# Sorting all five edge groups of layer 1 in a two-layer graph kernel, with dense work on x beside the first sort

## The reference, cut to what matters

```python
edge_index = jnp.stack([src, dst]); batch0 = jnp.zeros((6250,), jnp.int32)
h = relu(layernorm(x))
# first layer (layer 1 below)
agg = zeros_like(h).at[src].add(edge_attr)                  # 100000 rows of 256
q = (h @ Wq.T + bq).reshape(n, H, DH); k, v = u[batch] @ Wk.T + bk, u[batch] @ Wv.T + bv
w = softmax(sum(q * k, -1, keepdims=True) / sqrt(DH), axis=-1)
cond = (w * v).reshape(n, D) @ Wo.T + bo
x = x + relu(concat([h, agg, cond], 1) @ W1.T + b1) @ W2.T + b2
# second layer
h = relu(layernorm(x))
ht = relu(h @ W1 + b1); w = exp(w_param)
fsum = segment_sum(sigmoid(w * ht[src] + b_param), dst, 6250)   # rows gathered by src, summed by dst
s = clip(fsum, 1e-6, 0.9999999); c = (log(s / (1 - s)) - b_param) / w
bundle = concat([ht, c], 1) @ Wn + bn
out = x + relu(bundle / max(norm(bundle), 1e-12))
```

## Time and profile before

| | us |
|---|---|
| median of three timed runs | 2949.75 (2943.0 to 2951.38) |
| the profiled execution | 2918.7 |
| its span | 2917.0 |
| TensorE busy (share of the span) | 2107.8 (72%) |
| VectorE busy | 1824.2 (63%) |
| GpSimd busy | 1787.9 (61%) |
| ScalarE busy | 1288.0 (44%) |
| mean granted clock of TensorE | 0.836 |

### The profile page before, as it was taken

The page is one execution under the profiler, slowest core; times in us unless marked ns, Lnnn a source line. Parts: engine busy times, 40 slices in busy tenths (PEclk is TensorE's granted clock), DMA queues, the critical chain, the costliest instruction groups (busy, mean ns, idle before and its releaser), DMA issues.

```text
span 2917.0 us, 36909 instructions
## 1 busy us (share of the span) xinstructions
PE 2107.8 (72%) x9923; PEld 1483.2 (51%) x9923; DVE 1824.2 (63%) x4995; ACT 1288.0 (44%) x4284; POOL 1787.9 (61%) x1714
## 2 busy tenths in 40 slices
PE   1569976677776877867997576777776777676785
PEld 0457754454554554545776354445455455443474
DVE  1574434665775775767775476677577677552586
ACT  0124443335444634635346343643553553463554
POOL 1577777767666666664025666666667667666337
PEclk9778886779887988988998687997888888885798
DMA  9888878435433333332546333333333333333143
GB/s 383 236 174 179 174 120 243 112 91 145 120 89 89 92 89 88 92 90 63 177 157 231 91 87 89 90 92 90 90 90 91 90 90 91 91 92 92 47 156 113
DMA packets 175359, 357.77 MB, mean 123 GB/s; under 512 B 32444, under 2 KB 100822, under 8 KB 172581
## 3 DMA queue, kind: packets, MB, share of 16 engines
q0 software_dynamic: 93168, 219.39, 30.0%
q1 hardware_dynamic: 70791, 101.03, 10.7%
q10 hardware_dynamic: 11200, 35.00, 3.2%
HBM read 275.21 MB, written 93.19 MB: 126 GB/s over the span
## 4 chain that ended last, share of the span: by engine, by line
PE 46%; DVE 23%; issue 12%; another core or an unknown queue 9%; SPq 3%; ACT 2%; DVEq 1%; POOL 1%; DMA 1%; POOLq 0%; ACTq 0%
PE bank L1405 44%; DVE agg L1171 11%; DVE oh L1103 3%; DVE hits L1099 3%; DVE store L1095 2%; SPq L452 1%; DVEq L1163 1%; ACT oh L791 1%; DVE cum L1056 1%; PE bank L1568 1%; SPq L480 1%; DVE store L904 1%; DVE cum L1063 1%; ACT store L719 0%
## 5 line engine op out<-in xcount | busy, mean ns | idle before, releaser
L1405 PE MATMUL bank<-store,oh 125*128 125x157 f16 (+2 forms) x6770 | 1530.0, 376 | 550.4 <-issue 213.4
L1405 PEld LDWEIGHTS bank<-store,oh 125*128 125x128 f16 (+1 forms) x6770 | 1012.9, 174 | 1003.4 <-issue 522.8
L1171 DVE TENSOR_TENSOR agg<-bank,agg 128x256 f32 x1845 | 777.4, 421 | 500.3 <-PE bank L1405 221.0
L646 POOL DMA_INDIRECT store<-g_table,idx_all x785 | 771.1, 982 | 386.1 <-issue 189.2
L791 ACT ACTIVATE oh<-dist 128x128 f32<-128x128 f32 x1845 | 499.1, 301 | 1079.4 <-PE bank L1405 610.9
L646 POOL DMA_INDIRECT store<-in_edge_attr,idx_all x628 | 626.1, 997 | 288.7 <-issue 144.8
L783 ACT ACTIVATE dist<-iota,nloc_all 128x128 f32<-128x128 f32 x1845 | 582.6, 386 | 74.0 <-DVE nloc_all L1143 38.2
L1095 DVE TENSOR_TENSOR store<-iota,ttab 125x628 f16<-125x628 f16 x360 | 173.4, 482 | 302.5 <-remote 210.6
L620 POOL DMA_INDIRECT agg_copy<-agg x160 | 251.8, 1574 | 173.5 <-ACT agg L746 79.4
L1103 DVE TENSOR_TENSOR oh<-hits,v 125x512 f16<-125x512 f16 x720 | 289.7, 422 | 6.4
L1405 PE MATMUL bank<-agg 128*128 128x256 f32 (+2 forms) x480 | 128.2, 419 | 55.3 <-DVE agg L1192 43.9
(11 more groups left out here) (207 smaller groups left out, 1512.1 us busy)
## 6 DMA issues: line engine op xcount, KB each, us to landing
agg_copy<-store ACTq DMA_DIRECT2D x4, 6400.0 KB
agg<-in_edge_attr SPq DMA_DIRECT2D x39, 512.0 KB, 4.3
store<-in_x SPq DMA_DIRECT2D x72, 256.0 KB
agg_copy<-agg_copy POOLq DMA_DIRECT2D x16, 800.0 KB
store<-g_table,idx_all POOLq DMA_INDIRECT x785
store<-in_edge_attr,idx_all POOLq DMA_INDIRECT x628
pre_scratch<-store SPq DMA_DIRECT2D x25, 256.0 KB
agg<-agg_copy SPq DMA_DIRECT2D x25, 256.0 KB
```

What stands on the lines that cost most here:

```text
L646: gp.indirect_dma_start(out=store[:, at % RING * D:(at % RING + 1) * D], out_offset=None, in_=table_dram, in_offset=bass.IndirectOffsetOnA ...
L1171: dve.tensor_tensor(to, pt[n % TB][:, 0:D], to, ALU.add).wait_op(s_mm, n + 1, "sem-ge").then_inc(s_acc, 1)
L1405: return pe.matmul(o, l, r, start=start, stop=stop, skip_group_check=skip)
```

## The change

It does five things.

1. Layer 1 has five sorted groups and no scattered one (SPREAD goes, G1 = 5, SORTS = 10). All the buffers, transfers and instructions of the scatter and of the folds go.
2. Stage A has 27 blocks (START = NW + 2). The weights are prepared ahead of the first, so ahead of the sort too. Block b has the dense work of chunk b (b < 25) and an even share of the first sort's atoms.
3. x is loaded once for stage A, straight to `agg`, which holds it until GpSimd clears each chunk after its transpose. The normalisation coefficients are made by batches of five chunks (`ln_coefs`, `norms_ready`).
4. The product of ht with the upper half of Wn, with bn added by a product of ones, is made in 50 halves between the jobs of stage D (`upper_product`, at the steps of HT_STEPS: six in each of the first four groups, 26 in the last), copied out by ScalarE and stored as `q_dram`.
5. In stage E the lower half of Wn is scaled once by 1/w, `bundle_product` has two products a row block, VectorE adds the stored half and clamps, ScalarE takes squares with a fixed scale, the per-row maximum goes, and VectorE does the scaled relu nine chunks later (`positive`) in GpSimd's place.

The core of the diff:

```diff
-SPREAD = 1
-G1 = GROUPS - SPREAD
+G1 = GROUPS
...
-        BLOCKS = spread_over([1.0] * (WBLOCK + 1) + [2.0] * (FIRST - WBLOCK - 1) + [0.76] * (EBLKS - 2 - FIRST)) + [range(0)] * 2
+        BLOCKS = spread_over([1.0] * START)
+        HT_STEPS = [(g, t) for g in STAGES[1][:-1] for t in (50, 54, 58, 147, 151, 155)]
+        HT_STEPS += [(STAGES[1][-1], 4 + 6 * i) for i in range(2 * NW - len(HT_STEPS))]
+        HT_HALF = {at: divmod(i, 2) for i, at in enumerate(HT_STEPS)}
...   # SP, stage D
+            upper_load(0)
+            for g in STAGES[1]:
+                for t in range(TILES):
+                    if (g, t) in UPPER_STORES:
+                        upper_store(UPPER_STORES[g, t])
+                    if (g, t) in HT_HALF and HT_HALF[g, t][1] and HT_HALF[g, t][0] + 1 < NW:
+                        upper_load(HT_HALF[g, t][0] + 1)
+                    if PLACE_ATOM + 3 in atoms_at(1, g, t):
+                        column_starts(g + 1)
...   # GpSimd, stage A
+            for n in range(NW):
+                gp.wait_ge(s_tp, n + 1)
+                gp.memset(slot2k(agg, n), 0.0).then_inc(s_z, 1)
...   # ScalarE, stage A
+            weights_ready()
+            norms_ready(0)
+            norm_relu(0)
+            for b in range(START):
+                if 1 <= b <= NW:
+                    act.wait_ge(s_d, b)
+                    act.activation(soft[:, 1, (b - 1) % 2, :], soft[:, 0, (b - 1) % 2, :], ACT.Exp).then_inc(s_e, 1)
+                if b < NW:
+                    h_out(b)
+                if 1 <= b <= NW:
+                    weights_out(b - 1)
+                    pre_out(b - 1)
+                if b + 1 < NW:
+                    if (b + 1) % CHB == 0:
+                        norms_ready((b + 1) // CHB)
+                    norm_relu(b + 1)
...   # VectorE, stage A
+            weights_ready()
+            ln_coefs(0, 2 * CHB, 1)
+            for b in range(START):
                 atoms = BLOCKS[b]
                 half = len(atoms) // 2
+                if 1 <= b <= NW:
+                    weights(b - 1)
                 for k in atoms[:half]:
                     sort_atom(0, k)
+                if b < NW:
+                    scores(b)
                 for k in atoms[half:]:
                     sort_atom(0, k)
+                if b + CHB < NW:
+                    stats(b + CHB)
+                    if b % CHB == CHB - 1:
+                        dve.wait_ge(s_bn0, b + CHB + 1)
+                        ln_coefs(2 * (b + 1), 2 * (b + 1 + CHB), b // CHB + 2)
...   # TensorE, stage A
+            for b in range(START):
                 atoms = BLOCKS[b]
                 half = len(atoms) // 2
+                if b < NW:
+                    h_transpose(b)
+                if 1 <= b <= NW:
+                    weight_transpose(b - 1)
                 for k in atoms[:half]:
                     sort_atom(0, k)
+                if b < NW:
+                    h_product(b)
+                if 1 <= b <= NW:
+                    weighted(b - 1)
+                if b < NW:
+                    score_product(b)
                 for k in atoms[half:]:
                     sort_atom(0, k)
+
+            def upper_product(n, j):
+                pe.wait_ge(s_hl, 16 * (n + 1))
+                if n >= 2:
+                    pe.wait_ge(s_qo, n - 1)
+                to = (pA, pB)[n % 2][:, j * D:(j + 1) * D]
+                for k in range(KD):
+                    mm(to, w1bT[:, k * WIN + j * P:k * WIN + (j + 1) * P], wn[:, k, :], k == 0, False)
+                r = mm(to, ones[0:1, :], bnbc[0:1, :], False, True)
+                if j:
+                    r.then_inc(s_qp, 1)
...   # VectorE, stage E
             def bundle(n):
                 dve.wait_ge(s_bm, n + CHB + 1)
+                dve.wait_ge(s_xl[n % CHB], XLOADS + 16 * (n // CHB) + 16)
+                dve.tensor_tensor(agg[:, n * CH:(n + 1) * CH], pt[n % CHB % 2][:, :], slot2k(ring, CHB + n % CHB),
+                                  ALU.add).then_inc(s_bs, 1)
+                dve.wait_ge(s_bs, n + 1)
+                ts(agg[:, n * CH:(n + 1) * CH], agg[:, n * CH:(n + 1) * CH], BMAX, -BMAX, ALU.min, ALU.max).then_inc(s_bd, 1)
```

More of the change, by code:

```diff
@@ L1385, in _ @@
                     norm_out(n // CHB - 1)
+                if n >= OUT_LAG:
+                    positive(n - OUT_LAG)
             bundle(NW - 1)
-            scale(NW - 1)
+            for n in range(NW - OUT_LAG, LASTS):
+                positive(n)
             norm_in(CBODIES - 1)
```

574 lines of the change are left out of this document (158 added, 416 removed).

## The result

The changed kernel takes **3026.51 us** (median of four runs, 3021.69 to 3028.99) against 2946.38 (2942.52 to 2951.38) for the kernel before: a ratio of 1.0274, with a 95% interval of 1.0256 to 1.0291. The forecast was 3017 us, the range 2975 to 3065. The profiled execution took 3021.69 us, its span is 3019.6.

What follows compares the result with a forecast made beforehand. No one engine bounds the whole: TensorE paces the dense work, the ring of gathers the sorted groups. Terms -130 + 226 - 1.5 + 3 - 30 = +67.5 us gave 3017 us, range 2975 to 3065.

Steps and rivals of the forecast that it cites:

- Stage A: Start, first sort and dense work on x: without the scatter, gathers start near 304 us instead of 434.4, -130 us.
- The turn of 9.7 us: Dense loop of stage A: VectorE's 3.7 us and TensorE's 6.0 us per chunk run in series.
- Rival 1: Stage A's turn is TensorE's work alone, 7.0 us; gathers start at 222, total 2935 us; chance 0.07.
- rival 4: TensorE's clock falls in stage A; at 0.73 the turn is 10.9 us, total 3046 us; chance 0.14.
- The four coefficient places: Stage A, after chunks 4, 9, 14, 19: coefficients and a table load delay VectorE 5 us each, 20 us.
- Stage B: Layer 1's sorted groups: a fifth costs 231.5 us less about 5 for dropped fold transfers, +226 us.
- Stage C: Dense work between the layers: fold sums and loads go, only the head is gained, -1.5 us (0 to -5).
- Stage D: Layer 2's five sorted groups: the upper product added in their loops costs +3 us (-3 to +25).
- The ring of gathers hides it: Stage D: gathers pace each group, so the upper product's 75 us on TensorE are covered.
- Rival 2: Upper product's halves run in series in stage D: +75 to +87 us, 3089 us or more; chance 0.07.
- Stage E: The end: less VectorE work per chunk and a shorter tail, -30 us (-18 to -38).
- Rival 3: The end doesn't give its 30 us, as chunks wait for ScalarE's logarithms and table loads: 3047 us; chance 0.1.

Runs made afterwards that it cites:

- The filler: The changed kernel with five extra constant transposes on TensorE per chunk in stage A: 2678.2 us against 2695.59 on the same chip.
- the two other orders: Two kernels, each the changed kernel with one edit: weights' transpose moved behind the chunk product, 2682.71 us; all statistics and coefficients ahead of the loop, 2673.22 us.
- the orders together: The changed kernel with both the later weights' transpose and the statistics and coefficients ahead of the loop: 2997.69 us against 3027.08.

## Why the prediction was right, point by point

**Stage A (-130, came -124.3).** The weight preparation was put at 20 to 36 us and ran from 23.3 to 38.4. The first weights' reciprocal came at 50.3, the last at 301.7. The first scores came at 48.7 (forecast 44) and the last at 299.1 (294), so the loop took its 250 us, and 5 of the 6 us that the gathers came late are in the start. The turn of 9.7 us was right in its mechanism, VectorE and TensorE in series, and nearly in its sum: 9.76 to 9.79 in the even turns, 10.05 on average in the middle of the stage. The runs bear the mechanism out: taking the transpose out of the series gave turns down to 7.0, the rival's value for TensorE alone, and the gathers came 20 us earlier. Rival 1 with its 222 us was never near, since TensorE has other work between, and even with both costs gone it needs 8.0 a turn.

The clock was the weak step, and here luck helped. I took 0.88 from a stretch in which TensorE was full and applied it to one in which I had found it busy 6.9 of 9.7 us. It was 0.71 to 0.74: rival 4's condition came true. Its gathers at 333 did not, because its turn of 10.9 us was worked out with 5.3 us for TensorE at full clock and 3.7 for VectorE. TensorE's part is 4.8 at full clock and became 6.4 to 6.5 at the clock it was granted, VectorE's is 3.3 to 3.7. Work put too high and a clock put too high cancelled: with the right clock and the work as I had it the forecast would have been rival 4's. The filler shows a reserve of 21 us in stage A; each of the two other orders gives about as much, 20 and 25 us, and the orders together only 27.

The four coefficient places were put at 5 us each. VectorE's part of those turns is 7.9 to 8.5 us instead of 3.3, 4.5 to 5.2 more each. As whole turns they stand 6.4, 6.1, 4.3 and 4.3 us above the average of 10.05, 21 us for 20; the first two have a slower part of TensorE besides.

**Stage B (+226, in this pair +245.4).** The term was a group at 231.5 less 5 for the folds, which have no row behind them. The price by timed runs is 237.8, so the term was mis-sized by 6. Half of it I put down to the source: its length came from a profiled execution that was 28 us quicker than the median. Over nine groups that is 3 us a group, which I should have added, having noted the difference and put all differences on the median unscaled. That it lies in the groups is worked out, not shown: the middle groups of the changed kernel and of its variants on 2946 chips last 234 to 238 us, those of the kernel before, as profiled, 230.5 to 235.5. A second trace of the kernel before on a 2946 chip would tell, and the one that was meant to came from a 2670 chip. So the rival, that the changed kernel's groups are longer by their own doing, isn't excluded. The sign that I had given, groups of 230 to 233 us in B, did not come: the five are 232 to 236.

**Stage C (-1.5, came -4.8).** At the better end of its bounds.

**Stage D (+3, in this pair +21.2).** 9.6 us of it are the upper product's, within the bounds of -3 to +25 but not the +3 taken. The rest, 12 us, I put down to the quick profile of the kernel before as in B, five groups at 2 to 3 us, which is not shown either. In this pair a middle group of D grew by 3 to 6 us, on average 4.5: more than the 3 that I had called right, and once more than the 5 that I had called wrong; 1 to 2 us of that are the product's, by the run without it. "The ring of gathers hides it" is right on the 2670 chips (0.1 us between traces of one chip, 1.8 between those of the changed kernel and the kernel before on two) and only nearly right on the 2946 chips. Rival 2 (75 to 87 us in series) falls.

**Stage E (-30, came -34.9).** A chunk went from 4.8 to 3.96 us (forecast 3.7 to 4.2), the tail from 24 to 17.0 (forecast 17), and the clamp takes 0.43 (taken 0.5). VectorE doesn't wait for the stored product: of the bundle sums shown above, two follow the work before them without a gap, and the last waits 0.50 us for TensorE. Rival 3 falls.

**The sum.** With the two terms from timed runs: -124.3 + 237.8 + 9.6 - 4.8 - 34.9 = +83.4, against +80.1 of the medians. What is left over, 3 us, has the sign and about the size of the 5 us forecast for the folds, which no run takes by themselves. The forecast of +67.5 was low by 6 in A, 6 in the group and 7 in D, and high by 5 in E and 3 in C. These parts were in the range.

What the forecast didn't see is that its largest term differs from chip to chip. On a chip where a group takes 204 us the same change costs 24 us, 1%. Both ways it is slower, for the reason given: the scattering did the fifth group's work beside dense work and a first sort that need 310 us by themselves in the order written, and 283 to 290 in a better one.

## What to carry to other kernels

When two engines hand one small result back and forth inside a loop, write the turn as a sum of both engines' parts, look up what ran between them before, and move the consumer behind independent work; after that, look at the granted clock, since TensorE, where it waited here, also ran its own part slower (0.74 against 0.82 to 0.90 where it waited less or was given extra work). Split a change into the parts that share no stage: here the end and the hidden product gave 1.1% where they were taken alone, and the fifth group took it back. Before durations of one profiled execution go into a sum, compare its time with the median; the difference, spread over the stage that repeats, belongs into the term.

## What the hardware showed that I had not expected

- The same instructions take 2946 us on some chips and 2670 on others. The issue pace of gathers is the same, 1.25 us; on a 2946 chip it is interrupted, each time by up to 2.7 us for GpSimd and up to 5 for VectorE and ScalarE, and the granted clock is lower too (0.83 to 0.87 against 0.92 in the middle groups of D of the kernel before).
- Work that nobody reads made a kernel faster: 125 extra transposes in stage A, 17.4 us less in all.
- With the halves of the upper product TensorE's clock in the last group rose from 0.72 to 0.80, so that 154 more records cost 29 us and not the 39 that 26 halves at 1.5 us would make.
